# Unread identity products while TensorE waits, a narrow memset and first rows turned first, in a two-layer graph-attention and expert-mixture kernel

## What is computed

```python
x = x + elu(softmax(mask(leaky_relu(s1[:, None] + s2[None, :], 0.2))) @ h)     # h = layernorm(x) @ W, s1 = h @ a1, s2 = h @ a2
x = x + sum over the best 2 of 8 experts of w_e * (gelu(xn @ W1[e] + b1[e]) @ W2[e] + b2[e])
x = x + relu(softmax(mask(leaky_relu(..., 0.01))) @ h)                          # second graph layer, its own W and a
x = x + relu(relu(xn @ W1[e] + b1[e]) @ W2[e] + b2[e])                          # e = the best of 32 experts
```

## Time and profile before

| | |
|---|---|
| median of 3 runs | 1144.89 us (1144.57 to 1146.49) |
| the profiled execution | 1146.29 us, its span 1144.6 us |
| TensorE matmuls (PE) busy | 918.4 us, 80% |
| VectorE (DVE) busy | 790.8 us, 69% |
| ScalarE (ACT) busy | 699.9 us, 61% |
| GpSimd (POOL) busy | 774.0 us, 68% |
| granted TensorE clock, mean | 0.861 |

### The profile page before, as it was taken

How to read it: one execution, slowest core, us unless ns; L and a number is a source line. 1 busy time by engine, 2 the same in 40 slices (tenths; PEclk the granted TensorE clock), 3 DMA queues, 4 the chain that set the end, 5 groups by cost and what they waited for, 6 DMA issues and landing times. The chain is left out here.

```text
span 1144.6 us, 27026 instructions
## 1 busy us (share of the span) xinstructions
PE 918.4 (80%) x6709; PEld 815.7 (71%) x6709; DVE 790.8 (69%) x3511; ACT 699.9 (61%) x2364; POOL 774.0 (68%) x1039
## 2 busy tenths in 40 slices
PE   5988889887379999999996599999984377656683
PEld 4777778776279999999996488888873255435463
DVE  6689999998569999999996168888887122221122
ACT  3999999896055555555554599999981143323320
POOL 4447887777728777877878017777887366666665
PEclk9999999988589999999999799999995565775655
DMA  9234432213257777878772212233312343232200
GB/s 210 64 98 146 145 102 74 62 53 112 83 162 209 204 205 206 204 201 210 200 202 74 66 38 76 76 80 87 80 40 74 82 121 94 80 87 84 66 21 37
DMA packets 144906, 129.22 MB, mean 113 GB/s; under 512 B 26522, under 2 KB 116511, under 8 KB 144755
## 3 DMA queue, kind: packets, MB, share of 16 engines
q1 hardware_dynamic: 124114, 91.94, 31.9%
q0 software_dynamic: 17760, 34.20, 8.5%
q10 hardware_dynamic: 2880, 1.35, 0.4%
HBM read 82.74 MB, written 47.48 MB: 114 GB/s over the span
## 5 line engine op out<-in xcount | busy, mean ns | idle before, releaser
L546 POOL DMA_INDIRECT xs<-staged,dst x256 | 260.7, 1018 | 76.9 <-issue 68.3
L1258 ACT ACTIVATE hT<-bank,wt 128x128 f32<-128x128 f32 x620 | 177.1, 369 | 123.1 <-PE bank L1488 86.4
L619 POOL DMA_INDIRECT out<-oq,xq x144 | 145.0, 1007 | 96.4 <-DVE oq L1157 57.4
L597 POOL DMA_INDIRECT x2d<-ob,xi x155 | 164.0, 1058 | 42.8 <-issue 28.5
L1470 PE MATMUL bank<-xnT,wt 128*128 128x128 f32 x1240 | 167.5, 279 | 11.1 <-ACT hT L1258 10.0
L1488 PE MATMUL bank<-w2s,hT 128*128 x1240 | 166.3, 277 | 0.6 <-ACT hT L1258 0.5
L1470 PEld LDWEIGHTS bank<-xnT,wt 128*128 128x128 f32 x1240 | 152.9, 194 | 13.9 <-issue 13.3
L1488 PEld LDWEIGHTS bank<-w2s,hT 128*128 128x128 f32 x1240 | 151.5, 193 | 1.5 <-issue 1.1
L1157 DVE SCALAR_TENSOR_TENSOR oq<-bank,xq 128x512 f32<-128x512 f32 x36 | 24.9, 692 | 173.5 <-remote 95.8
L1207 ACT ACTIVATE p<-bank,nm 128x128 f32<-128x128 f32 x256 | 105.0, 411 | 17.6 <-DVE nm L792 14.4
L1305 ACT ACTIVATE xnqT<-bank 128x512 f32<-128x512 f32 x36 | 21.5, 596 | 153.0 <-PE bank L1357 70.8
(11 more groups left out here) (262 smaller groups left out, 2249.5 us busy)
## 6 DMA issues: line engine op xcount, KB each, us to landing
wt<-wpd SPq DMA_DIRECT2D x155, 258.0 KB
xi<-xs SPq DMA_DIRECT2D x155, 66.0 KB
xq<-xs SPq DMA_DIRECT2D x144, 66.0 KB
xb<-x2d SPq DMA_DIRECT2D x32, 258.0 KB
xb<-in_x SPq DMA_DIRECT2D x32, 256.0 KB
wpd<-w1c SPq DMA_DIRECT2D x56, 129.0 KB
xs<-staged,dst POOLq DMA_INDIRECT x256
x2d<-ob,xi POOLq DMA_INDIRECT x155
```

The lines of the kernel that those rows point to most:

```text
L546: pool.indirect_dma_start(out=xs[l], out_offset=bass.IndirectOffsetOnAxis(ap=dst[b % ND][:, c:c + 1], axis=0), in_=stag[s][:, q, 0:ROW], i ...
L597: pool.indirect_dma_start(out=x2d, out_offset=bass.IndirectOffsetOnAxis(ap=xi[t % NXI][:, ID:ID + 1].bitcast(U32), axis=0), in_=ob[:, t % ...
L619: pool.indirect_dma_start(out=orow, out_offset=bass.IndirectOffsetOnAxis(ap=xq[j % NXQ][:, q, ID:ID + 1].bitcast(U32), axis=0), in_=oq[j % ...
L1258: last = act.activation(hT[t % 2][:, j, :], HID[t % 2][:, j, :], ACT.Gelu, bias=wt[t % NW][:, c:c + 1])
```

## The change

Four things. `keep_running(bank, n)` issues n bf16 matmuls of the identity with the identity broadcast to 512 columns into a bank that nobody reads at that time. It stands at TensorE's start (14, after `identb`), at the end of graph layer one before the table's transpose (10, when the last `hg` is copied), after mixture one (36, then 30 more when the last `x2_rstd` is out) and before mixture two (30, when the scatters of layer two's last group but one have landed). GpSimd clears only column 32 of each expert in `vt` (128 x 32 elements). TensorE turns the first group's rows before the weight products, which move into `graph_weights` with one semaphore step for each layer and the second layer's product in bank 5. VectorE makes `cmat` before it waits for the loads, and copies each layer's weights with a semaphore step of its own; TensorE's first L1382 so waits for the first layer's three copies alone, and the second layer's are awaited before step 1's routing product writes to `SM`.

```diff
@@ -535,7 +535,7 @@
             pool.wait_ge(sem("pad"), 1)
             pool.memset(pad[:, ID:ID + 1].bitcast(I32), NOWHERE).then_inc(sem("pad"), 1)
 
-            pool.memset(vt[:, :, :], 0.0).then_inc(sem("vt_zero"), 1)
+            pool.memset(vt[:, :, H1:H1 + 1], 0.0).then_inc(sem("vt_zero"), 1)
             def scatter(n, half):
                 l, g = divmod(n, NG)
                 s, b = n % NS, OF_GROUP[n]
@@ -683,25 +683,23 @@
             stats(first_of_two(0), xb[0])
             for part in spread_parts(-1):
                 part()
-            dve.wait_ge(sem("graph_in"), 16 * 4)
             dve.wait_ge(sem("ident"), 1)
             dve.tensor_scalar(cmat[:, :], ident[:, :], -1.0 / P, None, ALU.add)
+            dve.wait_ge(sem("graph_in"), 16 * 4)
             for l in range(2):
                 w = wraw[l][:, 0:P].unsqueeze(1).broadcast_to([P, 2, P])
                 link(dve.tensor_tensor(wprod[:, l, :, :], w, arow[:, l, :, :], ALU.mult))
-                last = dve.reduce_sum(wraw[l][:, P:P + 2], wprod[:, l, :, :], AX.X)
-            last.then_inc(sem("wraw"), 1)
+                dve.reduce_sum(wraw[l][:, P:P + 2], wprod[:, l, :, :], AX.X).then_inc(sem("wraw"), 1)
             dve.wait_ge(sem("adj_in"), 16)
             link(dve.tensor_copy(adj_f[:, :], adj_i[:, :]))
             dve.tensor_scalar(mask[0][:, :], adj_f[:, :], 0.0, MASKED, ALU.is_le, ALU.mult)
             dve.tensor_scalar(mask[1][:, :], adj_f[:, :], 0.0, MASKED, ALU.is_equal, ALU.mult).then_inc(sem("mask"), 1)
-            dve.wait_ge(sem("wcat_ps"), 1)
             for l in range(2):
-                o = l * (P + 2)
-                dve.tensor_copy(wcat[l][:, :], SM[:, o:o + P])
-                dve.tensor_copy(wa1[l][:, :], SM[:, o + P:o + P + 1].broadcast_to([P, P]))
-                last = dve.tensor_copy(wa2[l][:, :], SM[:, o + P + 1:o + P + 2].broadcast_to([P, P]))
-            last.then_inc(sem("wcat"), 1)
+                after(dve, "wcat_ps", l)
+                w = (SM, AB[0])[l]
+                dve.tensor_copy(wcat[l][:, :], w[:, 0:P])
+                dve.tensor_copy(wa1[l][:, :], w[:, P:P + 1].broadcast_to([P, P]))
+                dve.tensor_copy(wa2[l][:, :], w[:, P + 1:P + 2].broadcast_to([P, P])).then_inc(sem("wcat"), 1)
 
             def routing_weights(part):
                 if part == 0:
@@ -1311,12 +1309,18 @@
 
         @block.tensor
         def _(pe):
-            pe.wait_ge(sem("wraw"), 1)
-            for l in range(2):
-                last = pe.matmul(SM[:, l * (P + 2):(l + 1) * (P + 2)], cmat[:, :], wraw[l][:, :], start=(l == 0), stop=(l == 1),
-                                 skip_group_check=True)
-            last.then_inc(sem("wcat_ps"), 1)
+            def keep_running(bank_, n):
+                for _ in range(n):
+                    pe.matmul(g4(bank_), identb[:, :], identb[:, :].unsqueeze(1).broadcast_to([P, G, P]), start=True, stop=True,
+                              skip_group_check=True)
+
             pe.wait_ge(sem("identb"), 1)
+            keep_running(HB, 14)
+
+            def graph_weights():
+                for l in range(2):
+                    after(pe, "wraw", l)
+                    pe.matmul((SM, AB[0])[l][:, 0:P + 2], cmat[:, :], wraw[l][:, :], start=True, stop=True).then_inc(sem("wcat_ps"), 1)
 
             def routing_weights(part):
                 if part == 0:
@@ -1418,6 +1422,10 @@
                         if l == 0 and 2 <= i < 8:
                             after(pe, "spare", i - 2)
                         turn(TP, xs_, "tx_ps")
+                    if l == 0 and i == 0:
+                        graph_weights()
+                    if l == 0 and i == 1:
+                        pe.wait_ge(sem("wcat"), 2)
                     if l == 0 and i in (1, 2):
                         routing_weights(i - 1)
                         first_bias(i - 1)
@@ -1448,6 +1456,9 @@
                     if l == 1 or i not in PART[0][2]:
                         rows_turned(n - 4)
                 w = 8 if l == 0 else 2
+                if l == 0:
+                    after(pe, "hg", NG - 1)
+                    keep_running(HB, 10)
                 pe.wait_ge(sem("tabf"), l + 1)
                 pe.transpose(SM[0:w, 0:P], tabf[l][:, :, :].rearrange("p k c -> p (k c)")[:, 0:w], ident[:, :]).then_inc(sem("tab_ps"), 1)
 
@@ -1489,8 +1500,14 @@
                                              start=(h == 0 and c == 0), stop=(h == 1 and c == 1), skip_group_check=True)
                     last.then_inc(sem("l2"), 1)
 
+            keep_running(SM, 36)
+            after(pe, "x2_rstd", len(TWOS) - 1)
+            keep_running(SM, 30)
             graph_layer(1)
             pe.wait_ge(sem("table"), 3)
+            m = 2 * NG - 2
+            pe.wait_ge(sem(f"scattered{m % NS}"), 16 * G * (m // NS + 1))
+            keep_running(SM, 30)
             pe.wait_ge(sem("v2_in"), 16 * 3)
             pe.wait_ge(sem("meet_in"), 16 * 3)
             for i in range(QUADS + 2):
```

## The result

The changed kernel takes **1139.06 us** in the median of 5 runs (1137.18 to 1141.01), the kernel before 1146.49 in 5 runs beside it; the ratio is 0.9944, 95% interval 0.9928 to 0.9959. So the change brings 0.56% by the ratio, which is 6.4 us (4.7 to 8.3 by the interval); the two medians lie 7.4 apart. I had forecast 1131.0, a gain of 14.1. The sign was right and the time lies in the range; the gain is about half of what I wrote. The profiled execution took 1139.06 us, its span 1137.3: 7.3 less than the 1144.6 of before.

The account below looks back on a forecast made before the run. It saw four stages with four limits: three engines in layer one, TensorE in mixture one, a TensorE at low clock in the last stage's first 19.1 us. Terms 4.8 + 0 + 3.3 + 6.0 = 14.1 us from 1144.89 gave 1131, range 1119 to 1140.

Parts of the forecast that it names:

- The start: Start of layer one: shorter cast, fewer copies awaited and a warm TensorE win 4.8 us (bounds 3.5 and 5.5).
- Rival (b): Layer one swallows the start's gain, as VectorE or a fixed-time load holds the loop: 1135.6 us; chance 0.12.
- The end of layer one: After layer one: the 10 products are hidden and bring nothing, 0 us (bounds 0 and -1).
- A lead carried whole through mixture one: Mixture one was to begin about 4.8 us earlier and be as long as before.
- Into layer two: Hand-over after mixture one: 66 products let TensorE start layer two's first group at full clock, 3.3 us (bounds 0 and 3.6).
- The last stage: Mixture two: 30 hidden products give a start at full clock, 6.0 us by the second output (bounds 0 and 12).
- the 2.4 to the first output: Last stage: a TensorE at full clock takes 2.4 us off up to the first output at 914.35.
- the 3.69 us gap: Last stage before the second output at 922.90: GpSimd starves 3.69 us; a faster group closes the gap.
- Rival (a): The last stage gives nothing, as unnamed waits or GpSimd's batches swallow the lead: 8.1 us gain, 1136.8; chance 0.18.
- (c): The warmth lasts in the last stage, so only GpSimd binds: up to 39 us more, 1092 or part; chance 0.08.
- (d): Products of the identity do not hold the clock, so batches end late: 4.8 us slower, 1149.7; chance 0.06.
- (e): The change does nothing: first rows and stages start as late as before; chance 0.03.

Follow-up runs that it names:

- e10: The changed kernel plus 3 products in each group of layer one from the ninth on; ratio to the kernel before 0.9942.
- b0: The kernel before, unaltered, run again in the second group on a quicker chip; 1091.78 us, ratio 0.9999.
- e7: The kernel before with the narrow memset alone, old order, no products; ratio to the kernel before 0.9974.
- e2: The kernel before with narrow memset and new order only, no products; ratio to the kernel before 0.9934.
- e5: The changed kernel with 38 for 30 products in layer two's second batch and 3 after the first turn; ratio to the kernel before 0.9911.
- e6: The changed kernel without the 30 products ahead of the last stage and their wait; ratio to the kernel before 0.9915.
- e8: The kernel before with the new order alone, wide memset kept, no products; ratio to the kernel before 0.9987.
- e14: The edits of e12 plus ScalarE's 12 fill issues moved behind mixture one's first six gelus, two each; ratio to the kernel before 0.9958.
- e13: The changed kernel with 60 instead of 30 products in the second batch ahead of layer two; ratio to the kernel before 0.9979.
- e11: The changed kernel plus products inside the first six steps of the last stage; ratio to the kernel before 0.9921.
- e12: The changed kernel with the edits of e9 and e11 together; ratio to the kernel before 0.9926.
- e3: The kernel before with only the 36 and 30 products ahead of layer two; ratio to the kernel before 0.9974.
- e9: The changed kernel with 38 for 30 products before layer two and more filling gaps in its first four groups; ratio to the kernel before 0.9892.
- e4: The kernel before with only the 30 products ahead of the last stage; ratio to the kernel before 0.9966.
- a0: The changed kernel, unaltered, run again in the second group on a quicker chip; ratio to the kernel before 0.9919.
- a1: The changed kernel, unaltered, as control of the third group on a quicker chip; ratio to the kernel before 0.9902.

## Why the prediction was right or wrong

**The start, 4.8 us (bounds 3.5 and 5.5): right.** 4.95 at the first matmul and 5.26 at the fill row. Over twelve profiles with the changed start and its 14 products (e10 left out) the fill row lies between 293.7 and 298.0, median 294.7; over four with the old one between 299.2 and 300.7. Of the 300.35 of b0 the memset alone takes 3.1 (e7), the order on top of it 1.2 (e2); the 14 products may be worth the 1.3 from there to the median, but by the timed runs (0.9934 without them, 0.9939 with) they are worth nothing, and in e5 and e6 the clock fell at 16.5 in spite of them. The cast and the copies that I summed are the gain, with one thing wrong in the picture: it is VectorE as a whole that stands beside the wide memset, not the cast (e8). Rival (b) falls: layer one carries the lead.

**The end of layer one, 0 (or -1): right.** Fill row to first gelu is 9.0 to 9.2 us with and without the 10 products on the four quicker chips (e14 left out), 18.7 to 19.3 on the others.

**A lead carried whole through mixture one: off by 1.4.** I let the lead pass between the stages unchanged. In the first pair 0.5 went before the first gelu, which is what ScalarE's 12 issues took longer, and 0.9 in mixture one. The full clock came 4.5 us after the first gelu before (324.0 against 319.5) and 6.4 after it in the changed kernel (321.2, 314.8). The six profiles from slower chips go with that: mixture one takes 299.6 to 299.8 us where the clock comes 4.5 to 4.8 us after the first gelu (before, e8, e13), and 300.7 to 301.1 where it comes 6.4 to 7.3 after it (the changed kernel, e11, e12). On the second chip nothing was lost (294.2 became 293.0), though there too the clock rose later in the changed kernel, 2.9 us after the first gelu against 0.2 before it; so on the quicker chips something else sets this stretch, and it is not known what. When the clock rises differs from run to run, and I had no term for it.

**Into layer two, 3.3 (bounds 0 and 3.6): 1.3 measured.** The step that failed is "TensorE then starts at the high level", carried over the first group. The turn did (0.66), the matmuls behind it did not: TensorE stands 1.7, 0.7 and then 1.3 us there, and the clock fell. Where the clock held (e3, e9, e12, e14) the stretch takes 220.3 to 220.7 us, without products 222.2 to 223.7, in the changed kernel 222.0 to 222.3. The sum of 3.3 was right for a clock that holds, against the trace that it was worked out from: on slower chips 223.6 became 220.3 (e12), 3.3. On the quicker ones it is worth 1.8 (b0 222.4, e9 220.6), and of the 1.3 of the unfilled hand-over only 0.1 is left (222.4 and 222.3). The rows show why the base is not the same: in b0 the clock rises by itself 23.0 us after the last gelu, in the kernel before of the forecast 25.6 us after it.

**The last stage, 6.0 (bounds 0 and 12): the term that failed.** In the first pair it gave 1.4 + 1.3 - 0.7 = 2.0. Of the 2.4 to the first output 1.4 came, because the clock fell again at 901.5 for 3.4 us; held (e11) it is 2.3. Of the 3.69 us gap 1.28 closed. I took the gap as a cold TensorE alone. On the quicker chips it is just that: 3.69 with the clock down (e4), none with it up (a0, a1, e5, e9), unless products inside the steps are in the way (e14). In the changed kernel of the first pair the second quad ran warm and the gap stayed at 2.41 by an unnamed wait, 1.8 us from the end of TensorE's products to VectorE's oq. I had seen such waits in the earlier trace rows but placed them behind this quad ("the gap before 922.90 comes earlier than all of them"). Rival (a), at 1136.8, names the cause and lies nearest to the 1139.06; I gave it 0.18. Its gain of 8.1 still holds the whole 3.3 for layer two. The rest of the distance is the base: I counted from 1144.89, and the kernel before took 1146.49 beside the changed one.

**The other rivals.** (c): on the quicker chips the last stage does run at GpSimd's 1.31 us per issue, but with the kernel before as well, so that is no gain of warmth. (d): the 66 products ran at 0.22 us each; identity products do hold the clock, and raise it too (7.2 us into the start, before 20.3; 894.7 ahead of the last stage, before 924.8). e13 shows its price to be real once a batch overruns. (e): excluded by the cast.

**The two rules of the Trainium skill.** The Trainium skill, TensorE: Matmul & The Clock Gate, Part 4 (PE-mode transpose), says that the full clock does not engage for transposes. The turns at 0.60 to 0.66 us, against 1.11 with the clock at 0.50, speak against it again. The same page of the Trainium skill, Part 1 (HAM oscillation), has DMA waits between bursts of matmuls put the engine back to the lower clock each time. The changed kernel's trace agrees in direction, 1.95 us at 635.10 behind gaps of 1.71 and 0.69; but e3, with gaps of 1.35 and 0.69, kept the clock, and the waits in the page's example are longer than all of these. I had used the rule against rival (c) and not against my own term for layer two, where it would have been a warning.

What stays open: what the unnamed waits are. They come in groups in which issues by ScalarE and SyncE are 2.3 to 2.6 times as long (12 in 16.56 against 6.47, 16 in 20.13 [SyncE, before] against 8.90 [a0_after]), they sit where an engine takes over from TensorE, and no run here removes them. Open too is whether a version beats the changed kernel: e11 and e12 have the lower ratio of the kind of chip that they ran on (0.9921 and 0.9926, the changed kernel 0.9944 in another group), e9 a lower one than its control by 0.001, all within the intervals.

## What to carry to other kernels

Products that keep TensorE busy pay only if no gap follows them before the work that they are meant for, and for the groups after it: here the fall came in eight of ten profiles with one gap of 1.3 us left open, and in none of three with all filled. Look for the next wait of about a microsecond behind the hand-over, for the loss can move there. Price a warm engine at the next bound, not at its own rate; here VectorE in layer one and GpSimd or an unnamed wait in the last stage took what TensorE won. And measure the parts alone: the narrow memset and the order gave 0.66% (0.44 to 0.89) without a single product, the whole change 0.81 to 0.98% on chips of the same kind.

## What the runs showed of the hardware that I had not expected

One kernel takes 1146 us in some groups of runs and 1094 in others, nearly 5% apart, with the same durations of matmuls and of GpSimd's issues (0.98 us), and with other times for issues of ScalarE and SyncE and unnamed waits where an engine follows TensorE. A cost read in one group, as my 6.0 us, need not exist in the next. And VectorE stands beside GpSimd's wide memset (4.38 us): the cast takes 4.24 us there in the kernel before and the masks 4.59 and 4.52 in e8, where beside the narrow memset they take 0.21, 0.23 and 0.22 (e7).
